# A one-core vision-transformer kernel: the transposes of the normalised tokens move to the end of a pipeline step, and one exponential moves ahead of their copy on ScalarE

## What is computed

```python
def reference(x, cls_tok, scharr, w_qkv, b_qkv, w_out, b_out, clip_x, clip_down, w_gate, w_up, w_down):
    h = tok(x, scharr)                      # grey image, two 3x3 edge filters, |.| summed / 2: (32, 256, 256)
    h = concatenate([broadcast(cls_tok), h], axis=1)             # (32, 257, 256)
    h = h + attn(layernorm(h), ...)         # causal, 16 heads, float32
    h = h + ffn(layernorm(h), ...)          # activations and weights fake-quantised to 8 bits
    return h

def attn(x, w_qkv, b_qkv, w_out, b_out):
    q, k, v = split(x @ w_qkv + b_qkv)      # 16 heads of 16
    att = softmax(where(causal, q @ k.T / 4, -inf))
    return (att @ v) @ w_out + b_out
```

## Time and profile before

| what | us |
|---|---|
| median of 3 timed runs | 1169.92 |
| lowest and highest of them | 1167.91, 1173.79 |
| profiled execution | 1166.12 |
| its span in the trace | 1164.4 |
| PE busy in the span | 949.2 (82%) |
| DVE busy | 806.9 (69%) |
| ACT busy | 686.8 (59%) |
| POOL busy | 537.5 (46%) |

### The profile page before, as it was taken

The page is one execution under the profiler, slowest core; times in us unless marked ns, Lnnn a source line. Parts: engine busy times, 40 slices in busy tenths (PEclk is TensorE's granted clock), DMA queues, the critical chain, the costliest instruction groups (busy, mean ns, idle before and its releaser), DMA issues. The chain is left out here.

```text
span 1164.4 us, 28062 instructions
## 1 busy us (share of the span) xinstructions
PE 949.2 (82%) x9584; PEld 681.1 (58%) x9584; DVE 806.9 (69%) x1969; ACT 686.8 (59%) x1171; POOL 537.5 (46%) x685
## 2 busy tenths in 40 slices
PE   2268899989989999899999999989988458885665
PEld 1045666666766767676676766767666333332544
DVE  1735566777776677777767777776666359998687
ACT  0154666666666666666666666666554237785785
POOL 5243555566556555655656565556443242220000
PEclk9988999999999999999999999999998769998888
DMA  3854455555555556555455655554322005501874
GB/s 86 233 133 112 126 138 152 149 133 148 149 133 129 137 154 150 138 150 143 126 135 148 154 135 150 148 131 105 101 62 62 12 1 199 199 1 50 271 231 137
DMA packets 156101, 152.90 MB, mean 131 GB/s; under 512 B 28263, under 2 KB 152458, under 8 KB 153994
## 3 DMA queue, kind: packets, MB, share of 16 engines
q1 hardware_dynamic: 156042, 152.14, 48.2%
HBM read 67.49 MB, written 28.35 MB: 82 GB/s over the span
## 5 line engine op out<-in xcount | busy, mean ns | idle before, releaser
L542 ACT ACTIVATE prob<-ST 128x772 f32<-128x772 f32 x256 | 209.2, 817 | 149.2 <-PE ST L956 143.9
L706 DVE TENSOR_REDUCE mneg<-SX 128x2 f32<-128x258 f32 x256 | 107.5, 420 | 212.3 <-PE SX L942 211.7
L939 PE MATMUL SX<-kst,qst 96*128 96x257 bf16 (+1 forms) x1024 | 159.9, 250 | 19.1 <-DMA qst<-qpart 10.4
L708 DVE TENSOR_REDUCE mneg<-SX 128x2 f32<-128x514 f32 x256 | 174.0, 680 | 0.0
L956 PE MATMUL ST<-qst,kst 98*128 98x256 bf16 (+2 forms) x1536 | 138.7, 223 | 15.5 <-DMA qst<-mpart 15.2
L942 PE MATMUL SX<-mask_s,ident_b 128*128 128x256 bf16 x512 | 142.4, 278 | 0.0
L451 POOL TENSOR_SCALAR_AFFINE_SELECT prob<-prob 128x1016 f32<-128x1016 f32 x128 | 142.2, 1111 | 0.0
L956 PEld LDWEIGHTS ST<-qst,kst 98*128 98x128 bf16 x1536 | 120.9, 99 | 33.8 <-DMA qst<-mpart 12.7
L939 PEld LDWEIGHTS SX<-kst,qst 96*128 96x128 bf16 x1024 | 91.7, 99 | 64.3 <-issue 28.2
L975 PE MATMUL G<-prob,vaug 128*32 128x256 f32 (+2 forms) x3072 | 117.3, 282 | 14.2 <-POOL prob L451 13.2
L975 PEld LDWEIGHTS G<-prob,vaug 128*32 128x32 f32 x3072 | 83.5, 111 | 48.1 <-POOL prob L451 19.7
(11 more groups left out here) (226 smaller groups left out, 1991.8 us busy)
## 6 DMA issues: line engine op xcount, KB each, us to landing
kst<-kpart SPq DMA_DIRECT2D x192, 128.5 KB, 2.5
xin<-in_x SPq DMA_DIRECT2D x96, 256.0 KB, 4.0
gst<-gray_dram SPq DMA_DIRECT2D x96, 256.0 KB
qst<-qpart SPq DMA_DIRECT2D x192, 128.0 KB, 2.4
h_dram<-hb SPq DMA_DIRECT2D x8, 1280.0 KB, 4.6
gray_dram<-gray SPq DMA_DIRECT2D x64, 128.0 KB, 2.7
result<-oy SPq DMA_DIRECT2D x32, 256.0 KB, 3.4
hb<-h_dram SPq DMA_DIRECT2D x5, 1280.0 KB, 6.5
```

The source lines that it names most:

```text
L542: nc.scalar.activation(prob[:, g % 2, 2 * (u % 2):2 * (u % 2) + 2, 0:QEND], ST[:, :, 0:QEND], ACT.Exp).then_inc(exp_done, 1)
L706: nc.vector.tensor_reduce(mneg[:, 0, u // 4, 0, at], SX[:, :, S0:S0 + P + 1], AX.X, ALU.max, negate=True)
L708: nc.vector.tensor_reduce(mneg[:, 1, u // 4, 0, at], SX[:, :, S1:S1 + T], AX.X, ALU.max, negate=True).then_inc(max_done, 1)
L939: mm(SX[:, r, at:at + k], qst[par][0:SR, 2 * u + r, P * t:P * t + P], kst[par][0:SR, 2 * u + r, 0:k], start=t == 1, stop=False)
```

## The change

On PE the four transposes of xhat leave slot 6, where they stood between `values` and `scores(7)`, and come behind `outputs` of group 0 at the end of slot 7, directly ahead of `turn_max(1)`. On ACT the exponential of part 2 comes ahead of the copy from M0 to xT. Nothing is added or removed.

```diff
@@ step of ScalarE @@
                 unnormalised(1)
                 exponential(bS, 1)
+                exponential(bS, 2)
                 if valid(bC):
                     wait(act, xT_done, bC, 1, 1)
                     wait(act, v_done, bP, 1, 1)
                     xt = M[0][:, :].rearrange("p (c t) -> p c t", c=KC)
                     nc.scalar.copy(xT[:, :, 0:1], xt[:, :, IMG - 1:IMG])
                     nc.scalar.copy(xT[:, :, 1:T], xt).then_inc(xT_ready, 1)
-                exponential(bS, 2)
@@ step of TensorE @@
                 values()
-                transposes()
                 scores(7)
                 scores_t(bS, par, 2)
                 outputs(bS, par, 0)
+                transposes()
                 turn_max(1)
```

## The result

The changed kernel takes 1190.8 us (median of 4 runs, 1188.1 to 1193.7) against 1171.9 for the kernel before (4 runs, 1167.9 to 1174.2; three of them are those of the table ahead of the prediction): a ratio of 1.0153 with a 95% interval of 1.0114 to 1.0192, so it is slower by 13 to 23 us. The span of the profiled execution grew from 1164.4 to 1186.4 us.

The account below looks back on a forecast made before the run. PE was nearly full, its 25.78 us period set by the loop through ACT's multiplications, POOL's grey and mask, and outputs(1). 28 x 0.75 - 1.85 = 19.15 us, added to 1169.4, gave 1188.5 us, range 1176 to 1197.

Parts of the forecast that it names:

- Part 1: Slot 6 on PE: scores(7) come 0.43 us earlier, but DVE is behind with its own work, so value 0.
- Part 2: Step's end on PE: transposes run inside the 0.64 us wait for DVE's maxima; PE's cost 0, 0.54 of wait left.
- Part 3: ACT at step's end: the copy waits for the late transposes, so the multiplications behind it begin 0.75 us later.
- Part 4: POOL's grey additions and mask shift by 0.75; outputs(1) on PE has no slack, so each step pays 0.75 us.
- The sum: Attention steps n = 4 to 31: 28 times 0.75, less 1.85 us of slack in six steps, gives 19.15 us.
- Hidden: Rival: the loop over queries, POOL's remainders and qst's landing hides the mask's delay; 1166 to 1173 if all hidden; chance 0.12.
- Faster: Rival: maxima(7) follow the earlier scores(7), bringing turn_max(1) and slot 0 forward; gain 6 to 12 us; chance 0.06.
- Dearer: Rival: shifted grey and mask on POOL collide with DVE operations, 0.42 more per step, sum 30.9, 1200 us; chance 0.06.
- The 0.1 for a change of operands: Extra PE time allowed for transposes behind outputs(0), with outputs' whole 0.90, making the shift 0.93 and the sum 24.

Follow-up runs that it names:

- The last experiment: Changed kernel against the kernel before, both with multiplications in ACT's wait and DVE's L850, L854, L856 moved into the next step's slot 1: 1159.9 against 1160.7 us.
- before_delayed: Kernel before with nothing moved, plus one idle copy of constants on ACT ahead of the multiplications: 1182.8 us, ratio 1.007 to 1.014.
- act_part_alone: Kernel before with only ACT's exponential of part 2 put ahead of the copy of xT, transposes left in slot 6: 1185.4 us, ratio 1.005 to 1.017.
- muls_in_acts_wait: Kernel before with ACT's three multiplications moved ahead of the copy of xT, where ACT idles for the transposes: 1214.1 us, ratio 1.027 to 1.037.

## Why the prediction was right, point by point

**Part 1 (earlier scores worth 0)**: held. Maxima(7) begin behind L842, with no wait, after the change too.

**Part 2 (the transposes fill the wait, PE's cost 0)**: held. They start 0.83 behind outputs(0) (0.82 predicted), and 0.49 of the wait for m_low is left (0.54). The last experiment shows the same without the trace: no difference between the two places beyond the scatter of the runs.

**Part 3 (multiplications 0.75 later)**: right in kind, a tenth too small. From outputs(0) to the multiplications is 2.06 instead of 2.00, since the transposes take 0.66 in their new place and not 0.60. From there to grey it is 1.85 (1.83 before) and on to the mask 2.73 (2.71 to 2.73 before). Together some 0.83 a step, and the period grew by 0.83 (26.473 less 25.646 before rounding).

**Part 4 (all of it reaches the period)**: held. Outputs(1) have a bracket of 0.8 to 0.9 in most steps where they had none, and later waits didn't take it up. The two runs that delay the mask otherwise, by 0.52 (before_delayed) and 0.55 (act_part_alone), lengthen the period by just that; the run that frees the mask gives all of it back in the period.

**The sum**: 28 steps by 0.75 less 1.85 gave 19.15 us. With the measured 0.83 it is 21.4, and the profiled spans differ by 22.0, all of it between the first grey addition and the last. The medians differ by 18.9, inside the interval of 13 to 23; that 19.15 is nearer to this is luck of the runs. The forecast of 1188.5 lies 2.3 below the measured 1190.8 because it started from 1169.4, the mean of the four runs then known, where the median is now 1171.9. The 0.1 for a change of operands, in the upper estimate of the shift, had no row behind it; measured, the transposes took 0.06 longer in their new place.

**The rivals.** *Hidden* is refuted by the brackets and by the delayed kernel before. *Faster* is refuted by the last pair of kernels. The general rule of the Trainium skill that it leaned on ("Perfetto Trace Analysis", section "Optimization Strategies"), to keep the matmul engine as highly utilised as possible, doesn't say that a gap must lie on the loop that sets the period. *Dearer* didn't occur in the change: L499 has a mean of 1.28 there and 1.27 before. But its mechanism is real, at twice the price that I gave it (0.9 a pair instead of 0.42), and in a place that I hadn't looked at when I wrote the expectation of muls_in_acts_wait.

What stays open: why the kernel with the mask first isn't faster than before. The wait for the DMA of the maxima is longer there, but what makes it so wasn't tried.

## What to carry to other kernels

A wait worth filling is one on the loop that sets the period. The profile's largest bracket need not be it, and the one that is may have no bracket at all: look for a consumer that starts at the same small distance (here 0.05 us) behind its producer in every step. Before an instruction is put in front of others on an in-order queue, follow every one of them to its reader on the other engines; here the copy was covered, and the multiplications behind it weren't. When work is moved into an idle stretch, look at what VectorE and GpSimd will then do side by side.

## What the runs showed of the hardware that was not expected

- A DVE operation that begins just behind a POOL addition waits for most of it: in the kernel with the multiplications in ACT's wait the first L850 of each pair takes 1.33 us and the second 0.40, a mean of 0.86, where the mean was 0.41 before. POOL's L501 beside it took 1.29, hardly more than its usual 1.27 (columns: count, busy us, mean ns, idle before):

```profile
L850 DVE TENSOR_SCALAR x<-h,ag,rstd 128x256 f32 x18 | 14.9, 864 | 0.0
```

- PE waits of 0.76 and 1.49 us within 3 us were followed by a stretch at a mean granted clock of 0.76, and waits of 0.76 and 1.51 in another step of the same execution by none: a PE that is otherwise busy can lose its clock behind waits this short, but not each time. In the changed kernel, with waits of 0.49, 0.59 (at the edge filter, 540.95) and 0.86 within some 6 us, the granted clock stayed at 1.00.
- Four transposes of 128x128 in float32 took 0.60 us behind `values` and 0.66 behind outputs of 32 columns.
